# Both halves of the first stage's Toeplitz tables loaded from DRAM instead of split on ScalarE and GpSimd, in a depthwise-convolution block in float32

## What is computed

```
y   = depthwise_conv7x7(x, dw_w) + dw_b                      # stage a
mu, var = mean and variance of y over the 96 channels        # stage a, running
h   = gelu(layernorm(y) @ w1 + b1)                           # stage b, 96 -> 384
h   = grn_gamma * (h * nx) + grn_beta + h                    # stage b
z   = x + (h @ w2 + b2)                                      # stage b
out = depthwise_conv3x3(floor_fixed(z), round_pow2(weight)) + floor_fixed(bias)   # stage c
```

## Time and profile before

| | before |
|---|---|
| median of 3 runs | 1137.85 us (1137.73 to 1139.84) |
| the profiled execution's own time | 1134.41 us |
| its span | 1132.6 us |
| busy share of the span: PE / DVE / ACT / POOL | 90% / 83% / 76% / 37% |
| stage a | 0 to about 401 us |
| stage b | about 401 to 930 us |
| stage c | about 930 to 1132.6 us |

### The profile page before, as it was taken

The page is one execution under the profiler, slowest core; times in us unless marked ns, Lnnn a source line. Parts: engine busy times, 40 slices in busy tenths (PEclk is TensorE's granted clock), DMA queues, the critical chain, the costliest instruction groups (busy, mean ns, idle before and its releaser), DMA issues.

```text
span 1132.6 us, 20794 instructions
## 1 busy us (share of the span) xinstructions
PE 1020.0 (90%) x5686; PEld 737.3 (65%) x5686; DVE 940.1 (83%) x1697; ACT 863.4 (76%) x1796; POOL 415.9 (37%) x331
## 2 busy tenths in 40 slices
PE   3898898888999928999999999999999967999996
PEld 3777777777777716666666666666666625767774
DVE  6899999999999955699999999999999674666665
ACT  3577777777777628788888888888888816999996
POOL 2567777777777615233232323223332000000000
PEclk9899999999999958899999999999999987999999
DMA  8566666666665254244444444444442329999996
GB/s 170 123 166 165 154 155 165 170 159 165 146 165 147 58 151 112 78 118 129 119 127 122 120 115 111 112 115 125 122 123 83 88 77 186 256 264 278 282 284 194
DMA packets 134167, 169.82 MB, mean 150 GB/s; under 512 B 11318, under 2 KB 129784, under 8 KB 129880
## 3 DMA queue, kind: packets, MB, share of 16 engines
q1 hardware_dynamic: 133216, 169.01, 57.3%
q10 hardware_dynamic: 920, 0.45, 0.2%
HBM read 110.92 MB, written 58.50 MB: 150 GB/s over the span
## 4 chain that ended last, share of the span: by engine, by line
PE 48%; issue 24%; ACT 10%; POOL 7%; DVE 6%; DMA 3%; POOLq 1%; SPq 1%; ACTq 0%; DVEq 0%
PE psum L636 21%; PE psum L626 6%; ACT arena L698 6%; PE psum L627 6%; PE psum L628 6%; PE psum L551 5%; POOL arena_r L464 4%; POOL arena L479 3%; ACT arena_r L683 3%; PE psum L619 2%; PE psum L533 1%; DMA arena<-lines_a 1%; PE psum L574 1%; ACT arena L744 1%; DVE arena L906 1%
## 5 line engine op out<-in xcount | busy, mean ns | idle before, releaser
L551 PE MATMUL psum<-arena_r 112*128 112x464 f32 x1536 | 375.9, 387 | 10.8 <-POOL arena_r L464 6.8
L551 PEld LDWEIGHTS psum<-arena_r 112*128 112x128 f32 x1536 | 276.9, 190 | 50.1 <-ACT arena L698 8.1
L636 PE MATMUL psum<-arena,w2s 128*96 128x448 f32 x672 | 271.3, 541 | 2.5 <-DVE w2s L977 2.5
L774 ACT ACTIVATE arena<-psum,b1g 128x448 f32<-128x448 f32 x336 | 200.5, 631 | 71.1 <-PE psum L628 71.1
L490 POOL TENSOR_TENSOR arena_r<-arena,arena_r 96x448 fp32r<-96x448 f32 x112 | 128.8, 1150 | 311.3 <-DVE arena_r L952 298.3
L698 ACT ACTIVATE arena<-psum,bias_a 64x224 f32<-64x224 f32 (+1 forms) x288 | 117.2, 442 | 89.6 <-PE psum L551 88.3
L636 PEld LDWEIGHTS psum<-arena,w2s 128*96 128x96 f32 x672 | 109.7, 163 | 113.8 <-issue 106.1
L881 DVE TENSOR_TENSOR arena_r<-psum,arena_r 112x224 fp32r<-112x224 f32 x384 | 127.1, 381 | 62.5 <-ACT arena_r L683 62.4
L533 PE MATMUL psum<-ident,arena 112*112 112x112 f32 x768 | 108.9, 277 | 63.2 <-DVE arena_r L881 36.0
L464 POOL TENSOR_TENSOR arena_r<-arena,arena_r 112x512 fp32r<-112x512 f32 x96 | 155.7, 1633 | 19.3 <-ACT arena_r L712 19.3
L479 POOL TENSOR_TENSOR arena<-arena 128x448 f32<-128x448 f32 x96 | 119.2, 1241 | 109.2 <-DVE arena L910 109.2
(11 more groups left out here) (97 smaller groups left out, 1097.3 us busy)
## 6 DMA issues: line engine op xcount, KB each, us to landing
arena<-lines_a SPq DMA_DIRECT2D x48, 448.0 KB
arena<-in_x_dram SPq DMA_DIRECT2D x48, 392.0 KB
y_scratch<-arena SPq DMA_DIRECT2D x48, 392.0 KB
arena_r<-y_scratch SPq DMA_DIRECT2D x16, 1176.0 KB, 7.6
arena<-in_x_dram SPq DMA_DIRECT2D x112, 168.0 KB, 2.5
z_scratch<-arena SPq DMA_DIRECT2D x112, 168.0 KB, 2.0
arena<-z_scratch SPq DMA_DIRECT2D x48, 392.0 KB
out_dram<-arena SPq DMA_DIRECT2D x48, 392.0 KB
```

What stands on the lines that cost most here:

```text
L551: mm = nc.tensor.matmul(p_conv[s % 2][:, 0:NCOL], w[:, p, s, TW * k:TW * k + TW], v[:, p, s, slot0 + k:slot0 + k + JP, :].rearrange("p j i ...
L636: mm = nc.tensor.matmul(p_o[k][0:C, 0:CH], w2s[:, p, m, :], hid[:, p, m, CH * t:CH * t + CH], start=(m == 0), stop=(m == MT - 1))
L774: nc.scalar.activation(hid[:, p, m, CH * t:CH * t + CH], p_h[m][:, 0:CH], ACT.Gelu, bias=b1g[:, m:m + 1]).then_inc(gelu_done, 1)
```

## The change

Two DRAM lines take the place of one: the setup on DVE splits the 96 lines of `la` into `lah` and `lal` (two instructions), and SP stores both. In stage a SP loads four table DMAs a batch (high and low, r = 0 and 1) straight into `toep_h` and `toep_l`; `toep`, `table_high` and `table_low` are gone, with the semaphores `a_th` and `a_tl`. Since the DMAs now write what PE reads, they wait until the batch that used the same buffers has been convolved (`a_conv`), and PE waits on the DMAs' own semaphore.

```
-    lines_a = nc.dram_tensor("lines_a", ...)
+    lines_h = nc.dram_tensor("lines_h", ...)
+    lines_l = nc.dram_tensor("lines_l", ...)
...
-        toep = conv(PAIR, 2, CB, KA * TW)
...
+        lah = conv_r(C, KA * TW)
+        lal = conv_r(C, KA * TW)
...
-            store_lines(lines_a, la, KA)
-            sp.wait_ge(lines_out, 3 * 16)
+            store_lines(lines_h, lah.bitcast(F32), KA)
+            store_lines(lines_l, lal.bitcast(F32), KA)
+            sp.wait_ge(lines_out, 6 * 16)
...
             def tables_a(b, s):
-                need(sp, stages["a"]["tl"], CB * (b - 1))
-                load_tables(stages["a"], lines_a, KA, toep, b, s)
+                need(sp, stages["a"]["conv"], CB * (b - 1))
+                load_tables(stages["a"], lines_h, KA, toep_h.bitcast(F32), b, s)
+                load_tables(stages["a"], lines_l, KA, toep_l.bitcast(F32), b, s)
...
-            def table_low(b, s, p):
-                pool.wait_ge(A["th"], CB * b + s + 1)
-                need(pool, A["conv"], CB * (b - 2) + s + 1)
-                pool.tensor_tensor(toep_l[:, p, s, :], toep[:, p, s, :], toep_h[:, p, s, :].bitcast(F32), ALU.subtract).then_inc(A["tl"], 1)
...
-                        if S is stages["a"]:
-                            pe.wait_ge(S["tl"], CB * b + CB)
-                        else:
-                            pe.wait_ge(S[f"t{p}"], 16 * (b - p) + 32)
+                        loads = 4 if S is stages["a"] else 2
+                        pe.wait_ge(S[f"t{p}"], 8 * loads * (b - p) + 16 * loads)
...
-                def table_high(b, s, p):
-                    if s == 0:
-                        act.wait_ge(S[f"t{p}"], 16 * (b - p) + 32)
-                    need(act, S["conv"], CB * (b - 2) + s + 1)
-                    nc.scalar.activation(toep_h[:, p, s, :], toep[:, p, s, :], ACT.Identity).then_inc(S["th"], 1)
...
-            dve.sem_inc(lines_made, 1)
+            link(dve.tensor_copy(lah, la))
+            dve.tensor_tensor(lal, la, lah.bitcast(F32), ALU.subtract).then_inc(lines_made, 1)
```

More of the change, by code:

```diff
@@ L96, in build @@
     KA, KC = 4, 2
-    lines_a = nc.dram_tensor("lines_a", (LPAD + C * TW * KA + TW + LPAD,), F32)
+    lines_h = nc.dram_tensor("lines_h", (LPAD + C * TW * KA + TW + LPAD,), F32)
+    lines_l = nc.dram_tensor("lines_l", (LPAD + C * TW * KA + TW + LPAD,), F32)
     lines_c = nc.dram_tensor("lines_c", (LPAD + C * TW * KC + TW + LPAD,), F32)
@@ L385, in _ @@
                 sp.wait_ge(stages["a"][f"st{s}"], 32 * NBODY)
-            sp.wait_ge(lines_out, 6 * 16)
+            sp.wait_ge(lines_out, 9 * 16)
             def load_y(i, p):
@@ L459, in _ @@
             pool.wait_ge(halo, 1)
-            def table_low(b, s, p):
-                pool.wait_ge(A["th"], CB * b + s + 1)
-                need(pool, A["conv"], CB * (b - 2) + s + 1)
-                pool.tensor_tensor(toep_l[:, p, s, :], toep[:, p, s, :], toep_h[:, p, s, :].bitcast(F32), ALU.subtract).then_inc(A["tl"], 1)
-            for s in range(CB):
-                table_low(0, s, 0)
             def add(it, first, last):
@@ L473, in add @@
                     n = CB * b + s
-                    if not (last and p == 1):
-                        for q in AHEAD[s]:
-                            table_low(b + 1, q, 1 - p)
                     pool.wait_ge(wel, 3 * n + 3)
@@ L706, in out_copy @@
                     nc.scalar.activation(rows_group(p, s), forwards(p_back[s % 2][0:CM], IG), ACT.Identity).then_inc(S["out"], 1)
-                def table_high(b, s, p):
-                    if s == 0:
-                        act.wait_ge(S[f"t{p}"], 16 * (b - p) + 32)
-                    need(act, S["conv"], CB * (b - 2) + s + 1)
-                    nc.scalar.activation(toep_h[:, p, s, :], toep[:, p, s, :], ACT.Identity).then_inc(S["th"], 1)
                 for s in range(G):
                     xt_copy(0, s, 0)
-                if rows_too:
-                    for s in range(CB):
-                        table_high(0, s, 0)
                 def body(it, first, last):
@@ L726, in body @@
                                     xt_copy(b + 1, q, 1 - p)
-                                    if rows_too:
-                                        table_high(b + 1, q, 1 - p)
                             yt_copy(b, s, p)
```

## The result

| | before | after |
|---|---|---|
| median | 1138.51 us (1137.73 to 1139.84, 4 runs) | 1242.34 us (1237.93 to 1244.49, 4 runs) |
| span of the profiled execution | 1132.6 us | 1240.5 us |
| busy share PE / DVE / ACT / POOL | 90 / 83 / 76 / 37% | 86 / 67 / 65 / 20% |

The ratio after to before is 1.0906, with a 95% interval of 1.0874 to 1.0938: 9.1% slower. The forecast was 1182 us with a range of 1146 to 1200. The direction and the place were right, the size was not.

The account below looks back on a forecast made before the run. POOL's table splits, slowing DVE, were taken to set 15.6 us a batch in stage a; the late store makes it 17.8, 20 x 2.2 = +44 us, other parts 0: 1137.85 + 44 = 1182 us, range 1146 to 1200.

Parts of the forecast that it names:

- What bounds the kernel before: Stage a: POOL's table splits slow DVE and set 15.6 us a batch; left to the engines, 14.0 us.
- What it adds and what it moves: Stage a: 0.918 MB more a batch; tables wait for convolution, the store queues behind them; a batch takes 17.8 us.
- the signs: Changed profile: table issues every 17 to 18.5 us, ACT waiting 6 to 8 us a batch, DMA share about 0.85.
- It holds for b = 3 to 22, 20 batches: Stage a: the batches that the late store lengthens, 2.2 us each, +44 us.
- The head: Kernel's start: later tables and rows against no splits and a shorter PE stop; 0, within 4 us either way.
- D: Stage a: time from a batch's beginning until its queued store lands, 12.4 us, bounds 10.8 to 13.1.
- T(b): Stage a: moment when the last channel of batch b-1 is convolved and batch b begins.
- two tables and store, issue to last byte: 8.2 us: SP's queue in stage a: 1.72 MB, read from an earlier trace's transfer windows, takes 8.2 us.
- The bound from above, 13.1: Store's landing in stage a: each pair of tables takes 4.9 us; 18.5 us a batch, +58 us in all.
- T(b+1) = T(b) + D + 5.4: Stage a: after the store lands, ACT's copies and hops take 2.5 us, PE's channel 3 0.1 + 2.8 us.
- rival 2: Stage a: TensorE's clock falls once a batch in PE's new stops, 2.4 us x 20 = +48, 1230 us; chance 0.05.
- Rival 1: Stage a: the store lands within 8.6 us of batch start, PE sets 14.0 us a batch, 1106 us; chance 0.11.

Follow-up runs that it names:

- 12 small matmuls: Changed kernel with 12 small matmuls (128x48) added on PE at step 2 ahead of the products, to fill its stop for `out_copy`: 1228.65 us, ratio 1.0829.
- 22 small matmuls: Changed kernel with 22 small matmuls (128x48) added on PE at step 2 ahead of the products, to fill its stop for `out_copy`: 1252.77 us, ratio 1.1029.
- store first: Changed kernel with SP issuing the store of batch b-3 ahead of the wait for the tables and of the tables: 1127.45 us, ratio 0.9884.

## Why the prediction was wrong

**What bounds the kernel before: right.** Line 908 of DVE (889 now) fell from 1452 to 684 ns with the splits gone, where 0.69 us was read from the last batch. PE's own pace of 14.0 us a batch shows where nothing else waits: in the first of the two batches of the run with the late wait and the store ahead of the tables.

**What it adds and what it moves: right.** Four tables, the store and the rows go out in a burst as a batch begins, ACT waits for the store 165.3 / 20 = 8.3 us a batch (I said 6 to 8), and this decides the time. The experiments bear it out from three sides: the same bytes in the old order are harmless in the steady part, the new order with half the bytes costs nothing against the kernel before (15.4 us a batch against 15.6), and the store ahead of the tables removes the wait. Of the signs, the table issues come every 20.3 to 20.8 us and not every 17 to 18.5, and the DMA share is 0.67 and not 0.85.

**"It holds for b = 3 to 22, 20 batches": right.** The head was put at 0 within 4 us and is +1.5, and by the terms that were named: PE's first product comes 6.5 us later (29.51 us instead of 23.06), and the stop of 4.5 us is one of 1.5 us, behind which the clock stays up.

**"The store lands D after T(b), D = 12.4 us": the first step that failed.** D is 13.6 us in the mean of 19 batches (13.24 in the one shown: 231.90 against a batch begun 0.15 us before 218.81). The terms for the wake and for two more tables stand. The failing term is "two tables and store, issue to last byte: 8.2 us": that was the end of the bytes in the windows, and with half the bytes the same transfers took 9.3 us until ACT went on. What fills the 1.1 us between the two was not shown; the bytes and the release were seen in different runs. The sum with this term is 0.15 + 9.3 + 4.2 = 13.7 us, against 13.6 measured. The bound from above, 13.1, had the same fault: D = 13.6 by itself gives 20 x 3.4 = 68 us and 1206, above the range. Cost against the forecast: 1.2 us x 20 = 24 us.

**"T(b+1) = T(b) + D + 5.4": the second step that failed.** From the landing to the next batch are 7.0 us in the mean. At full clock they are 5.2 (12 small matmuls), so the working was right, 0.2 us too high, for the clock that it assumed. I named the fall of the clock as rival 2, priced it well (2.4 us a batch, 1230 us; measured are 1.8) and gave it 0.05, for two reasons that both failed. I put the longest stop at some 2 us; with the later landing it is 2.9 to 4.1. And I argued from two rows that a stop of 1.27 us leaves the clock and one of 4.5 us lowers it, as if the length of the stop decided. With half the bytes it fell behind a stop of 1.63 us in one batch and not behind one of 1.65 in another, and with 22 small matmuls it fell in seven batches in which PE had been busy for at least 5 us. A stop that comes once in every batch, with little else known of it, should have had the even chance and not the small one. Cost: 1.6 x 20 = 32 us.

Together that is the 2.8 us by which a batch (20.6 us) missed 17.8, 20 x 2.8 = 56 us; the exact batches give 99.4 - 44 = 55.4. The whole miss is 60 us: 55.4, the head's 1.5, stage c's 8.0, less the 1.0 us between them and less the 3.4 us that the sum added between profile and median.

**Rival 1, the store in time,** did not happen: four tables and the store moved at the rate of the earlier trace rows, not at that of stage c, 270 GB/s. From 219 to 223 us the burst ran at 201 GB/s and from 223 to 234 us at 233, input rows among them:

```profile
219.00:223.00 4.00, 3.85 (x30) 3.15 (x29) 2.87 (x7) 2.84 (x9) 1.73 (x2) 1.00 0.73 201
223.00:234.00 11.00, 7.70 (x48) 5.90 (x48) 3.12 (x7) 3.05 (x9) 1.69 (x2) 0.90 0.92 233
```

## What to carry to other kernels

When loads no longer fill a staging buffer but the buffer that PE reads, their wait moves from "copied out" to "used up", which comes later; look at what stands behind this wait in the same DMA queue, a store above all, and ask when it must have landed. Read the length of a transfer from its issue to the instruction that it releases (9.3 us here for two tables and a store), not to its last byte (8.2 us). And where a change puts a new stop of a few microseconds into TensorE's path once per iteration, price the slower clock behind it in the main forecast: here the stops were 2.9 to 4.1 us, and in each of the 19 batches the channel behind took 4.4 to 5.0 us instead of 2.8.

## What the runs showed of the hardware

- ACT went on 9.3 us after the first issue of two table loads and a store, about 1.1 us later than the last byte that the earlier trace rows show for the same transfers in another run.
- The granted clock fell from its full to its lower level with stops of PE of 2.9 to 4.1 us in each of the 19 batches of the changed kernel from 73.09 us on; behind stops of 1.63 to 1.66 us in three of eight batches with half the bytes; behind 0.91 to 0.92 us in six of eleven batches with 12 small matmuls; and in seven batches with 22, PE having been busy for at least 5 us. The channel that followed took 4.0 to 5.0 us instead of 2.8. So the length of the last stop does not by itself tell whether it falls; what does stays open here.
- The changed kernel's batches lie close together, 20.3 to 20.8 us in all but the first. Channel 3 took 4.51 to 4.74 us in the ten in which ACT went on 13.2 to 13.5 us after the start, and 4.37 to 4.66 us in the eight with 13.7 to 13.9 us. Whether the fall of the clock sets this rhythm was not tried.
- One DMA queue moved 230 GB/s in stage a of "store first" with tables, rows and stores mixed, at a share of 0.92, against 159 before at a share of 0.64.
- Stage c of one and the same program took 208.7 us in one execution and 200.9 in another.
